# A four-stage Flamingo block on one core: joined lead maxima, and query projections in a bank of the maxima's ring

## The reference

```python
def _L0_ffn_ref(x, router_w, router_b, W1, b1, W2, b2):      # 8 experts of width 128, the best 2 count
    router_logits = x @ router_w + router_b
    routing_weights = jax.nn.softmax(router_logits, axis=-1)
    top_k_weights, top_k_indices = jax.lax.top_k(routing_weights, TOP_K)
    top_k_weights = top_k_weights / jnp.sum(top_k_weights, axis=-1, keepdims=True)
    ...
    h1 = jax.nn.gelu(jnp.einsum('btd,nde->btne', x, W1) + b1, approximate=False)
    out_per_expert = jnp.einsum('btne,nef->btnf', h1, W2) + b2
    return jnp.sum(out_per_expert * routing_mask[..., None], axis=-2)

def _L1_xattn_ref(x, context, Wq, bq, Wk, bk, Wv, bv, Wo, bo):   # 16 heads of 16 features
    ...
    attn = jax.nn.softmax(jnp.einsum('bhnd,bhmd->bhnm', q, k) * scale, axis=-1)
    out = jnp.einsum('bhnm,bhmd->bhnd', attn, v)
    return out.transpose(0, 2, 1, 3).reshape(B, N, C) @ Wo.T + bo

x = x + jnp.tanh(g_xattn[0]) * _L0_xattn_ref(ctx_1024, _layernorm(x), mask, ...)   # 16 heads of 64 features
x = x + jnp.tanh(g_ffn[0]) * _L0_ffn_ref(_layernorm(x), ...)
x = x + jnp.tanh(g_xattn[1]) * _L1_xattn_ref(_layernorm(x), ctx_1024, ...)
x = x + jnp.tanh(g_ffn[1]) * _L1_ffn_ref(_layernorm(x), ...)                       # quantised gated network
```

## Time and profile before

| | us |
|---|---|
| median of 3 runs | 3196.07 |
| lowest and highest run | 3194.3 and 3197.39 |
| the profiled execution, its own time | 3199.99 |
| its span (first to last instruction) | 3198.1 |
| mean granted TensorE clock in it | 0.985 of full speed |
| PE busy in the span | 2946.9 (92%) |
| DVE busy | 2420.5 (76%) |
| POOL busy | 2112.9 (66%) |
| ACT busy | 1816.6 (57%) |

### The profile page before, as it was taken

The page is one execution under the profiler, slowest core; times in us unless marked ns, Lnnn a source line. Parts: engine busy times, 40 slices in busy tenths (PEclk is TensorE's granted clock), DMA queues, the critical chain, the costliest instruction groups (busy, mean ns, idle before and its releaser), DMA issues. The chain is left out here.

```text
span 3198.1 us, 53588 instructions
## 1 busy us (share of the span) xinstructions
PE 2946.9 (92%) x21744; PEld 1087.4 (34%) x21744; DVE 2420.5 (76%) x2983; ACT 1816.6 (57%) x2032; POOL 2112.9 (66%) x1024
## 2 busy tenths in 40 slices
PE   6899999999999999999999999999888799999988
PEld 3233333333333333333333333322454233333235
DVE  8777787677777767777776777787446788888878
ACT  5555555455455545544555554554454588888865
POOL 5787988898898889789888988999432211111114
PEclk9999999999999999999999999999999899999989
DMA  2000000000000000000000000000110100000000
GB/s 64 6 1 1 1 8 1 1 8 1 1 1 8 1 1 7 1 1 4 4 1 1 3 1 1 33 1 1 39 32 6 51 8 8 7 6 7 6 1 27
DMA packets 24616, 28.73 MB, mean 9 GB/s; under 512 B 6511, under 2 KB 21296, under 8 KB 24370
## 3 DMA queue, kind: packets, MB, share of 16 engines
q1 hardware_dynamic: 24370, 25.31, 2.8%
HBM read 17.42 MB, written 2.10 MB: 6 GB/s over the span
## 5 line engine op out<-in xcount | busy, mean ns | idle before, releaser
L385 POOL TENSOR_TENSOR a_acc<-a_acc,a_prob 128x1024 f32<-128x1024 f32 x697 | 1713.8, 2459 | 297.4 <-ACT a_prob L531 214.6
L531 ACT ACTIVATE a_prob<-slot,a_mask_bias 128x1024 f32<-128x1024 f32 x928 | 987.5, 1113 | 734.4 <-PE slot L1034 719.1
L671 DVE TENSOR_REDUCE a_part_max<-wide 128x2 f32<-128x1024 f32 x880 | 1068.3, 1214 | 432.7 <-PE wide L1005 432.0
L1334 ACT ACTIVATE front_arena<-slot,a_mask_bias 128x1024 f32<-128x1024 f32 x416 | 455.7, 1116 | 70.9 <-PE slot L1521 58.1
L1049 PE MATMUL bank<-a_prob,a_val 128*64 128x512 f32 x1856 | 447.9, 604 | 0.2 <-ACT a_prob L531 0.2
L1049 PE MATMUL bank<-a_prob,front_arena 128*64 128x512 f32 x1856 | 447.6, 604 | 0.0
L1375 DVE TENSOR_REDUCE a_part_max<-wide 128x1 f32<-128x512 f32 x475 | 306.7, 680 | 28.0 <-PE wide L1509 13.3
L1034 PE MATMUL slot<-front_arena 64*128 64x512 f16 x1856 | 276.2, 376 | 0.3 <-DVE a_shift L688 0.3
L1303 POOL TENSOR_TENSOR x_res<-a_gated,x_res 128x512 f32<-128x512 f32 x32 | 40.9, 1278 | 342.0 <-ACT a_gated L1346 342.0
L1535 PE MATMUL bank<-front_arena,a_val 128*32 128x256 f32 x3328 | 262.7, 392 | 0.1
L1005 PE MATMUL wide<-a_k_hi,a_q_hi 64*128 64x512 f16 (+1 forms) x1024 | 179.0, 362 | 61.8 <-DVE a_part_max L671 58.1
(11 more groups left out here) (437 smaller groups left out, 3717.5 us busy)
## 6 DMA issues: line engine op xcount, KB each, us to landing
a_w_staged<-in_w SPq DMA_DIRECT2D x8, 384.0 KB, 3.2
x_res<-in_x SPq DMA_DIRECT2D x4, 512.0 KB, 6.4
out_x<-x_res SPq DMA_DIRECT2D x16, 128.0 KB, 1.7
a_q_raw<-a_hi SPq DMA_DIRECT2D x112, 16.0 KB, 1.8
front_arena<-in_ctxt SPq DMA_DIRECT2D x1, 1601.0 KB, 6.7
front_arena<-in_w1a SPq DMA_DIRECT2D x4, 384.5 KB, 5.6
a_acc<-in_ctx SPq DMA_DIRECT2D x3, 512.0 KB, 8.6
a_k_op<-front_arena SPq DMA_DIRECT2D x24, 52.0 KB, 2.2
```

The costliest lines, as they stand in the source:

```text
L385: nc.gpsimd.tensor_tensor(acc, before, prob[:, k % R, :], ALU.add).then_inc(added_p, 1)
L531: nc.scalar.activation(prob[:, k % R, :], m.slot[k % 2][:, :], ACT.Exp, bias=mbias[:, t:t + 1]).then_inc(probs_ready, 1)
L671: nc.vector.reduce_max(part_max[:, w % 2, :, j, c], pairs, AX.X).then_inc(max_used, 1)
L1334: nc.scalar.activation(prob[:, k % R, :], slot(("scores", w, s))[:, :], ACT.Exp, bias=mbias[:, t:t + 1]).then_inc(probs_ready, 1)
```

## The change

Six things change.

1. The first attention and the second no longer clear their semaphores or hold the second barrier when they end. The middle stage clears its own and the first attention's, the last stage its own and the second attention's. Two clears and two barriers go, and the two that stay clear more.
2. In the cross stage the projections are formed in a bank of the maxima's ring, which has one more use in each of 14 units, and no longer in a slot of the scores. `read_n` counts the ring's readers on DVE without the projections.
3. In the cross stage DVE scales the output bias in step 8 of unit 0, no longer ahead of its first maximum. POOL's wait for it moves to where POOL uses it.
4. In the middle stage the lead pairs take both halves of `wide`, and one `reduce_max` of 128x1024 reads both. The second layer adds up in `bank[0]` and `bank[1]` instead. The two tasks of step 31 are issued on PE after the whole second layer of step 31, and on DVE one stands after the last block's statistics and one after its scaling.
5. The eight fills of `k_op` with ones move from DVE to POOL. Four stand ahead of and between the weight splits `w_split(2)` and `w_split(3)`, and four after the last expert's split, ahead of the first `y_low`.
6. On ACT `w_high(3)` stands ahead of the exponential of the routing, and no longer after it and `evacuate(10)`.

The core of the diff:

```diff
-    def __init__(self, nc, tag):
-        self.nc, self.tag, self.all = nc, tag, []
+    used = []
+
+    def __init__(self, nc, tag, clear):
+        self.nc, self.tag, self.all, self.clear = nc, tag, [], clear
...
+        self.used.extend(self.all)
+        if kind is None and self.clear:
+
+            self.nc.clear_and_free_semaphores(self.used)
             self.nc.all_engine_barrier()
+            self.used.clear()
...
-    with Semaphores(nc, "a0") as sem, ExitStack() as ctx:
+    with Semaphores(nc, "a0", clear=False) as sem, ExitStack() as ctx:
...
-                if job_of(w, s) is not None:
-                    order.append(("proj", job_of(w, s)))
...
+                if job_of(w, s) is not None:
+                    uses.append(("proj", job_of(w, s)))
...
+        read_n = {what: n for n, what in enumerate([what for what in uses if what[0] != "proj"])}
...
-            pool.wait_ge(prep, 1)
...
+                    pool.wait_ge(prep, 1)
                     for t in range(NX):
                         nc.gpsimd.tensor_tensor(m.x[:, t, :], m.x[:, t, :], bos[:, :], ALU.add).then_inc(bias_added, 1)
...
-                src = slot(("proj", p))[:, 0:QB]
+                src = bank(("proj", p))
...
-            dve.wait_ge(bias_loaded, 16)
-            nc.vector.tensor_scalar(bos[:, :], bo[:, :], m.tg[:, a.gate:a.gate + 1], None, ALU.mult).then_inc(prep, 1)
...
+                    if w == 0 and s == a.den_at:
+                        dve.wait_ge(bias_loaded, 16)
+                        nc.vector.tensor_scalar(bos[:, :], bo[:, :], m.tg[:, a.gate:a.gate + 1], None, ALU.mult).then_inc(prep, 1)
...
-                if n >= a.banks:
-                    pe.wait_ge(ring_used, n - a.banks + 1)
+                for own in uses[max(n - a.banks - 1, 0):max(n - a.banks + 1, 0)]:
+                    if own[0] == "proj":
+                        pe.wait_ge(evacuated, own[1] - a.ahead + 1)
+                    else:
+                        pe.wait_ge(ring_used, read_n[own] + 1)
 
             def project(p):
                 g, u = divmod(p, NU)
-                free_slot(("proj", p))
-                out = slot(("proj", p))
+                free_bank(("proj", p))
+                out = bank(("proj", p))
...
-        for step, count in [(17, 2), (18, 2), (20, 2)] + [(s, 3) for s in (22, 23, 24, 25, 26, 28, 29)] + [(30, 2), (31, 2)]:
+        for step, count in [(17, 2), (18, 2), (20, 2)] + [(s, 3) for s in (22, 23, 24, 25, 26, 28, 29)] + [(30, 2)]:
             self.tasks_at[step] = list(range(n, n + count))
             n += count
-        assert n == self.lead.lead and self.tasks_at[29][-1] >= self.lead.tasks - 1
+        self.tasks_end = list(range(n, self.lead.lead))
+        assert self.tasks_at[29][-1] >= self.lead.tasks - 1
...
-        obank = lambda z: m.wide[:, z * 512:z * 512 + 512]
-        jbank = lambda p: obank(p % 2) if p // 2 % 2 == 0 else m.bank[p % 2][:, :]
-        tbank = lambda r, n: sbank(n) if r == 0 else hbank(n) if n >= DC * (NB - 1) else m.bank[n % 2][:, :]
+        obank = lambda z: m.bank[z][:, :]
+        lbank = lambda z: m.wide[:, z * 512:z * 512 + 512]
+        jbank = lambda p: lbank(p % 2) if p // 2 % 2 == 0 else obank(p % 2)
+        tbank = lambda r, n: sbank(n) if r == 0 else hbank(n) if n >= DC * (NB - 1) else lbank(n % 2)
...
+            def ones_of(g):
+                for z in range(a.pairs):
+                    nc.gpsimd.memset(keep.k_op[g][z][:, :], 1.0).then_inc(k_ones, 1)
...
             pool.wait_ge(lo_done, DC * NB)
+            ones_of(0)
             w_split(2)
+            ones_of(1)
+            w_split(3)
             nc.gpsimd.memset(wt_h[:, :], 0.0).then_inc(wt_zeroed, 1)
-            w_split(3)
             nc.gpsimd.memset(wt_l[:, :], 0.0).then_inc(wt_zeroed, 1)
...
+            for g in range(2, a.groups):
+                ones_of(g)
             for n in range(STEPS):
                 y_low(n)
...
+            w_high(3)
             act.wait_ge(shifted, 1)
             nc.scalar.activation(flat(lg), flat(lg), ACT.Exp).then_inc(exp_done, 1)
             evacuate(10)
-            w_high(3)
             evacuate(11)
...
-            for g in range(a.groups):
-                for z in range(a.pairs):
-                    nc.vector.memset(keep.k_op[g][z][:, :], 1.0).then_inc(k_ones, 1)
...
-                for h in range(2):
-                    src = m.bank[h][:, :]
-                    if i < lead.tasks - lead.pairs:
-                        z, jc = divmod(i, lead.blocks * lead.full)
-                        j, c = divmod(jc, lead.full)
-                        nc.vector.reduce_max(keep.part_max[:, w, 2 * z + h, j:j + 1, c], src, AX.X).then_inc(task_used, 1)
-                    else:
-                        z = i - (lead.tasks - lead.pairs)
-                        tails = src[:, 0:lead.blocks * lead.tail].rearrange("p (j n) -> p j n", j=lead.blocks)
-                        nc.vector.reduce_max(keep.part_max[:, w, 2 * z + h, :, lead.full], tails, AX.X).then_inc(task_used, 1)
+                both = m.wide[:, :].rearrange("p (h n) -> p h n", h=2)
+                if i < lead.tasks - lead.pairs:
+                    z, jc = divmod(i, lead.blocks * lead.full)
+                    j, c = divmod(jc, lead.full)
+                    nc.vector.reduce_max(keep.part_max[:, w, 2 * z:2 * z + 2, j, c], both, AX.X).then_inc(task_used, 1)
+                else:
+                    z = i - (lead.tasks - lead.pairs)
+                    tails = both[:, :, 0:lead.blocks * lead.tail].rearrange("p h (j n) -> p h j n", j=lead.blocks)
+                    nc.vector.reduce_max(keep.part_max[:, w, 2 * z:2 * z + 2, :, lead.full], tails, AX.X).then_inc(task_used, 1)
...
+            task(a.tasks_end[0])
             scale(1, NB - 1)
+            task(a.tasks_end[1])
             x_low(1, NB - 1)
...
-                    pe.wait_ge(task_used, 2 * (n + 1))
+                    pe.wait_ge(task_used, n + 1)
...
-                        ins = nc.tensor.matmul(m.bank[h][:, at:at + width_k], keep.q_op[z][r, w * QB + j * P:w * QB + (j + 1) * P],
+                        ins = nc.tensor.matmul(lbank(h)[:, at:at + width_k], keep.q_op[z][r, w * QB + j * P:w * QB + (j + 1) * P],
...
-                if n + 1 == STEPS and len(own) > 1:
-                    task(own[1])
                 if len(own) > 2:
                     task(own[2])
                 second_layer(n, 1)
+            for task_n in a.tasks_end:
+                task(task_n)
             turn(1, NB - 1)
```

More of the change, by code:

```diff
@@ L52, in __exit__ @@
     def __exit__(self, kind, *rest):
-        if kind is None:
-            self.nc.clear_and_free_semaphores(self.all)
+        self.used.extend(self.all)
+        if kind is None and self.clear:
+            self.nc.clear_and_free_semaphores(self.used)
             self.nc.all_engine_barrier()
+            self.used.clear()
 class Memory:
@@ L1180, in stage_cross @@
     LAID = 16 * 3 * G // a.pairs
-    with Semaphores(nc, "a1") as sem, ExitStack() as ctx:
+    with Semaphores(nc, "a1", clear=False) as sem, ExitStack() as ctx:
         def sb(name, shape, dt=FP32):
@@ L1261, in lay_shift @@
                 u = w % NU
-                sp.wait_ge(ring_used, use_n["turn", w] + 1)
+                sp.wait_ge(ring_used, read_n["turn", w] + 1)
                 if w > 1:
@@ L1366, in task @@
                 w, i = divmod(n, a.tasks)
-                dve.wait_ge(ring_ready, use_n["max", n, 1] + 1)
+                dve.wait_ge(ring_ready, read_n["max", n, 1] + 1)
                 if i == 0 and w > 2:
@@ L1388, in shift_of @@
             def shift_of(w):
-                dve.wait_ge(ring_ready, use_n["turn", w] + 1)
+                dve.wait_ge(ring_ready, read_n["turn", w] + 1)
                 if w > 1:
@@ L1420, in divide @@
             def divide(w):
-                dve.wait_ge(ring_ready, use_n["spread", w] + 1)
+                dve.wait_ge(ring_ready, read_n["spread", w] + 1)
                 dve.wait_ge(raw_ready, w + 1)
@@ L1468, in freed @@
                     return probs_ready, what[1] * S + what[2] + 1
-                if what[0] == "proj":
-                    return evacuated, what[1] - a.ahead + 1
                 return gated_ready, 2 * what[1] + what[2] + 1
@@ L1547, in spread @@
                 free_bank(("spread", w))
-                pe.wait_ge(ring_used, use_n["den", w] + 1)
+                pe.wait_ge(ring_used, read_n["den", w] + 1)
                 for j in range(a.blocks):
@@ L1563, in outputs @@
                 free_slot(("out", w, z))
-                pe.wait_ge(ring_used, use_n["spread", w] + 1)
+                pe.wait_ge(ring_used, read_n["spread", w] + 1)
                 pe.wait_ge(wo_loaded, 16)
@@ L1699, in stage_middle @@
     NB, STEPS, W, NC = a.nb, a.steps, 3 * DC * P, len(a.chunks)
-    with Semaphores(nc, "mid") as sem, ExitStack() as ctx:
+    with Semaphores(nc, "mid", clear=True) as sem, ExitStack() as ctx:
         def sb(name, shape, dt=FP32):
@@ L1762, in stage_middle @@
```

(13 more changed lines are left out.)

12 lines of the change are left out of this document (6 added, 6 removed).

## The result

The changed kernel takes **3204.61 us** (median of 8 runs, 3203.01 to 3206.17), the kernel before 3196.16 beside it. The ratio is 1.0026, with a 95% interval from 1.0016 to 1.0037: 8.4 us slower, where 14.2 us less had been forecast, and outside the range.

What follows compares the result with a forecast made beforehand. PE was taken to set the cross stage's pace and to wait for ACT and DVE elsewhere. Terms 0.9 + 8.1 + 0 + 1.8 + 0.2 + 3.3 − 0.1 + 0 = 14.2 us off 3196.07 gave 3181.9, range 3175.0 to 3189.5.

Steps and rivals of the forecast that it cites:

- Projection in the ring: Cross stage: forming projections in a bank of the maxima's ring keeps matmuls and waits the same; 0 us.
- The slower rival: Cross stage: ACT empties the projection late and PE's task waits, up to 1.5 us in 14 units; 3202.9 us, chance 0.04.
- The test that I had named for a wrong forecast: Signs of error included a cross-stage unit longer or shorter by over 0.1 us than 36.8 us.
- Fills leave DVE: Before the expert loop: earlier logits and exponential end PE's 6.28 us wait, so the loop starts about 8.1 us earlier.
- The rival in which another chain takes half of it: Before the expert loop: key rows or low parts of keys take half the routing gain; 3186 us, chance 0.15.
- Fills come to POOL: Middle stage: the 11.8 us of fills on POOL, 1.47 us each, are not on the path; 0 us.
- the rival of dear fills: Middle stage: POOL's fills take 4.0 us each, delaying w_split(3) and the first y_low; 3192.7 us, chance 0.07.
- Joined lead pairs and the tail: Expert loop: one reduction per pair saves some 0.08 us, 1.8 us over 23 pairs; the loop's tail saves 0.2.
- Cross start: Start of cross stage: the first maximum no longer waits for the bias DMA, saving 3.3 us; step 8 costs 0.1.
- Seams: Stage seams: two clears and barriers go, 1.8 us, of which some 0.9 comes back; saved 0.9 us.
- The sum: Whole kernel: all terms together save 14.2 us, from 3196.07 to 3181.9 us.

Runs made afterwards that it cites:

- e11: The changed kernel without the ring move: projections stay in a slot and free_bank has its single wait; 3183.09 us, ratio 0.9957.
- e4: The kernel before with only the projection moved to a bank of the ring, and one wait where both owners are maxima; 3196.02 us, ratio 1.0000.
- e1: The changed kernel, with free_bank dropping the first of its two waits where both are for maxima; 3181.49 us, ratio 0.9960.
- e5: The kernel before with only the fills moved to POOL and w_high(3) put ahead of the exponential; 3189.53 us, ratio 0.9977.
- e6: The kernel before with only the joined lead pairs and the two last tasks behind the second layer; 3193.73 us, ratio 0.9995.
- e7: The kernel before with only the output bias scaling moved to step 8 of unit 0; 3190.2 us, ratio 0.9984.
- e3: The kernel before with one more wait, for an older slot release, ahead of each scores pair of the cross stage; 3195.99 us, ratio 1.0001.
- e8: The kernel before with only the deferred semaphore clears; 3195.85 us, ratio 0.9998.
- e2: The kernel before with one more wait per cross-stage task, for an older read, written ahead of the blocking wait; 3213.6 us, ratio 1.0060.
- e10: The kernel before with one more wait per cross-stage task, for an older read, written behind the blocking wait; 3198.19 us, ratio 1.0006.
- e9: The kernel before with two more waits per cross-stage task, both for older reads on the same counter; 3216.77 us, ratio 1.0067.

## Why the prediction was wrong, point by point

**The step that failed** is one sentence under *Projection in the ring*: "Same matmuls, same number of waits." The matmuls are the same. The waits are not: the diff replaces one wait by a loop over two owners, in a function that each task of the cross stage calls, and I read it as part of the projection's bookkeeping and priced only the 14 projections. The term stood at 0. By the length of a unit it is (38.18 − 36.80) × 14 = 19.3 us, and against e11, at an equal clock, it measured 19.9. The rest of that term was right by e4: emptying the projection is no problem, and there is no gain, though a unit is 0.09 us longer.

**The slower rival** gave 3202.9, close to the time measured, by a mechanism that isn't there. ACT does not hold the ring (e1 and e4 have the same projections in the same bank and a unit of 36.89). Its price, up to 1.5 us in each of 14 units, came from PE's slack, and the true one is of that size by chance. The test that I had named for a wrong forecast, a unit longer by over 0.1 us, was the right place to look.

**Fills leave DVE** (8.1): right in mechanism and in size, 7.3 by e5's comparison, 8.4 in its rows and 7.6 in the profile after. One figure of the working is off by a little: from 2327.25 to 2320.4 the exponential gains 6.85 us and not 6.65. The exponential is bound by ACT's own table load, as worked out; the wait of 6.28 us and ACT's 8.57 are gone. The rival in which another chain takes half of it falls: the loop still begins on the same wait of 1.31 us for DVE, no longer one.

```profile
2317.93 1.28 ACT L1931 ACT_TABLE_LOAD   x1
2319.22 0.31 ACT L1931 ACTIVATE mid_logits<-mid_logits 128x128 f32<-128x128 f32 x1
...
2350.03 0.38 PE L2248 MATMUL slot<-mid_wt_hi,mid_pick 128*128 128x512 f16 x1 [1.31 <-DVE mid_k_lo L2021]
```

**Fills come to POOL** (0): right. Two fills last 2.91 us, four 5.76, so 1.45 each, where 1.47 had been worked out from POOL's longer fill. That is the time DVE needed for the same fill, and the rival of dear fills falls (its own sum gives 3192.9 and not 3192.7).

```profile
2314.18 2.91 POOL L1835 MEMSET a_k_op<- 128x1664 f16 x2
2317.99 1.16 POOL L1824 TENSOR_TENSOR front_arena<-front_arena 128x512 f16<-128x512 f32 x1 [0.90 <-ACT front_wq_hi L1890]
...
2342.36 5.76 POOL L1835 MEMSET a_k_op<- 128x1664 f16 x4
```

POOL even waits for ACT ahead of `w_split(3)`, so the fills were not in its way. The estimate by the rule in the Trainium skill, "GPSIMD Engine Reference", section "Key points", 2.9 us a fill, was off by a factor of two. Nor did fills slow DVE's small sums: the one of 128x128 that began at 2320.17, beside a zero fill of POOL's (2319.72 to 2321.52), took the 0.29 us of a sum with POOL at rest.

**Joined lead pairs and the tail** (2.0): not shown in its size, and probably too high. The row-to-row saving is 0.07 us a pair, as forecast, and the comparison of e6 gives 1.6 with an interval that holds 0. But the stretch itself was only 0.4 us shorter in e6. The 1.5 us of the changed kernel prove nothing: its loop ran at a granted clock of 1.00 and the kernel before's at 0.98, and e7, with separate pairs and also at 1.00, took 151.0 us against the changed kernel's 151.3, of which 0.5 is the longer seam.

**Cross start** (3.2): right in mechanism and, as far as can be told, in size. DVE's first maximum started 0.6 us behind PE's first pair (2501.95, 2501.31). e7's 5.1 us has 3.2 well inside its interval (1.9 to 8.3), and at a like clock the profiles give about 3 (e5 against e11). The forecast took the clock of 0.50 in this stretch as the kernel's own; e3, whose code is the same up to this stage, read 0.78 there, with a unit 0 that was 3.3 us shorter (36.7 and 40.0), as much as the edit itself is worth. It follows a tail of the loop in which PE was busy 5.06 of 15.7 us at a clock of 0.61 in the kernel before. What sets it from one execution to the next no run here shows.

**Seams** (0.9): right in the rows. PE started 0.13 us behind the first barrier and not 0.99, and the third seam is 0.6 us shorter. The later clears cost 0.5 and 0.2 us of that, so 0.8 is left. The comparison of e8 can't resolve it.

**The sum** of the other parts was right: 14.2 forecast, 14.9 by e1's medians (3196.39 − 3181.49) and 13.5 by e11's. By the ratios it is 12.8 and 13.7, with intervals some 5 us to either side, so the agreement is closer than the measurement can vouch for. One term that I did not see as a term turned it round.

## What to carry to other kernels

Read a diff for what each engine is issued, waits included, and count the calls of every function whose body changes, not the cases it was changed for. In a loop where one engine's read releases the next matmul, wait once, on the latest event, or write the wait that blocks first, so that it goes with the matmul. A rotation whose owners signal on different counters needs two waits only where they do differ.

## What the runs showed of the hardware

- A wait in an instruction of its own lasts 51 ns on PE's queue in every row (369 of 369). Where it is the wait that blocks, in the loop that sets the pace, it cost 0.07 to 0.08 us a step, 1.37 us a unit (e2). The same number with a fulfilled wait cost nothing (e10), nor did 398 at the scores (e3).
- Of two waits ahead of a matmul the one written last gets the instruction (e2, e10). A third goes into that same instruction, in 355 of 383, and added 0.18 us a unit (e9).
- GpSimd fills 128x1664 float16 in 1.45 us, as VectorE does.
- With the same code up to there, the granted clock in the first 18.7 us of the cross stage was 0.51 in one profile and 0.78 in another, and unit 0 took 40.0 and 36.7 us (before, e3).
- Clearing the semaphores of two stages at once takes nearly as long as clearing them apart (767 ns against 442 and 352), so deferring a clear saves the barrier alone.
